# A transformer block's expert layer: every token through all eight experts, or each token's rows sent to its two

## The chip, the cores and the metric

The program runs on one core of a Trainium2 chip. The core has a matrix engine (TensorE, PE in the rows, its weight loads PEld), three engines for elementwise work (VectorE or DVE, ScalarE or ACT, GpSimd or POOL), and SyncE (SP), which issues transfers. The metric is the device time of one execution in microseconds, lower is better. The kernel before took 1424.11 us as the median of three runs (1423.81 to 1424.6).

## The reference

Two layers, each an attention and a feed-forward part with a residual. Only the last part, the mixture of experts of layer 1, is changed. It works on 32 x 128 = 4096 tokens of 128 numbers:

```python
gate_out = jnp.einsum('bsd,ed->bse', x, Wg)            # x: layer norm of the tokens
top_v, top_i = jax.lax.top_k(gate_out, K)              # K = 2 of E = 8 experts
probs = jax.nn.softmax(top_v, axis=-1)
for e in range(E):
    w_e = jnp.sum(probs * (top_i == e), axis=-1)       # 0 for 6 of the 8 experts
    h1 = jnp.einsum('bsd,hd->bsh', x, W1[e])           # H = 256
    h2 = jnp.einsum('bsd,hd->bsh', x, W2[e])
    g = h1 * jax.nn.sigmoid(h1) * h2
    out = out + jnp.einsum('bsh,dh->bsd', g, W3[e]) * w_e[..., None]
x = x + jnp.tanh(g_ffn[1]) * out
```

## The kernel before

The kernel is a row of stages: `setup`, `split_transposed` and `project0`, `attention0`, `feed_forward0`, a second `split_transposed`, `attention1`, a third `split_transposed`, `mixture`. Each stage is one block of instruction streams, one for each engine that has work in it. At its end all five engines meet at a barrier (line 89 of the helper `Memory`), SyncE too, also where it had nothing to do. Within a stage semaphores alone order the engines.

A matrix product is made in half precision three times over (high part by high, high by low, low by high), so each fp32 operand is split into a high and a low fp16 part.

The third `split_transposed` (1098.6 to about 1120 us) normalises the tokens on VectorE, turns 128 x 128 blocks on TensorE and leaves them in `xh` and `xl`, features on the partitions. `mixture` takes eight chunks of 512 tokens (CH = 4 sequences), and for each chunk all eight experts. For one chunk and expert, TensorE makes 12 products of 512 columns (`rise`, lines 1628 to 1630), ScalarE the tanh and the high part, VectorE two products (lines 1753 and 1761), GpSimd the low part (line 1583), and TensorE 24 products of 128 columns (`fall`, line 1642). VectorE weighs the result by the gate, which is zero for six experts of eight (line 1771), and GpSimd adds it to `X` (line 1578). The gate of the next chunk is worked out on VectorE between two experts. SyncE only stores the finished chunks (line 1605). Everything stays in the on-chip memory, and the loops over the chunks are hardware loops.

SyncE's queue is empty from the end of `setup` to `attention1`, whose transposes (lines 1219 and 1222) move fp16 tiles within the on-chip memory. GpSimd issues no transfer in this kernel.

## Time and profile before

| | |
|---|---|
| median of three runs | 1424.11 us |
| the profiled execution: its own time | 1424.81 us |
| its span in the trace | 1423.0 us |
| TensorE busy, mean granted clock | 1213.8 us (85%), 0.883 |
| VectorE, ScalarE, GpSimd busy | 1075.0, 928.7, 855.5 us |
| data moved by transfers | 30.97 MB |

The span is the time from the first to the last instruction in the trace, 1.8 us less than the execution's own time. A busy engine is not always at its peak: matmuls overlap, so an engine that is 85% busy can have room. Times in the rows are microseconds from the span's start.

### The profile page before, as it was taken

What the parts mean: (1) busy time and instruction counts of PE and PEld (TensorE: products, weight loads), DVE (VectorE), ACT (ScalarE), POOL (GpSimd) and SP (SyncE); (2) the same over time, 40 slices, a digit from 0 to 9 for tenths busy, and PEclk for the clock granted to TensorE, in tenths of its full rate; (3) what the DMA queues carried; (4) which work ended last, traced back from release to release, by engine and by line L of the source; (5) the groups of instructions that cost most, each with busy time, mean ns of one, the idle gap of its engine ahead of it and who ended that gap; (6) DMA issues with size and microseconds to landing.
All of it is one profiled execution on the core that took longest, in us unless ns stands there. A gap on an engine that the chain in (4) does not pass through costs nothing. (4 is left out here: it accounts for less than half of the span.)

```text
span 1423.0 us, 39532 instructions
## 1 busy us (share of the span) xinstructions
PE 1213.8 (85%) x14773; PEld 910.6 (64%) x14773; DVE 1075.0 (76%) x2878; ACT 928.7 (65%) x1858; POOL 855.5 (60%) x823
## 2 busy tenths in 40 slices
PE   1578999958994599999999999999994688888887
PEld 1445777745663388878787878787874355555555
DVE  5888666666988766676868676867774799999996
ACT  0678888845663488878787878787872445554554
POOL 0251888852115366666666666666663477777778
PEclk9678555558996699999999999999997699999998
DMA  9100000000000011112211121112111000000000
GB/s 234 46 1 1 2 3 2 3 1 1 1 1 1 1 24 32 32 32 31 28 29 32 32 32 32 28 30 29 32 32 23 1 1 9 8 7 7 7 8 16
DMA packets 93785, 30.97 MB, mean 22 GB/s; under 512 B 78227, under 2 KB 91963, under 8 KB 93627
## 3 DMA queue, kind: packets, MB, share of 16 engines
q1 hardware_dynamic: 82587, 25.40, 8.8%
q10 hardware_dynamic: 11040, 3.42, 1.1%
q8 instruction: 106, 1.74, 0.5%
q14 instruction: 52, 0.43, 0.1%
HBM read 9.92 MB, written 2.10 MB: 8 GB/s over the span
## 5 line engine op out<-in xcount | busy, mean ns | idle before, releaser
L1167 POOL TENSOR_TENSOR attention_pl_l<-attention_probs_l,attention_ph_l 128x512 f16<-128x512 f32 x128 | 148.1, 1157 | 181.0 <-ACT attention_ph_l L1337 181.0
L1401 DVE TENSOR_REDUCE attention_negmax<-bank 128x2 f16<-128x410 f32 x256 | 137.7, 579 | 136.5 <-PE bank L1246 136.3
L1583 POOL TENSOR_TENSOR mixture_hidden_l<-mixture_hidden,mixture_hidden_h 128x512 f16<-128x512 f32 x128 | 148.2, 1158 | 74.9 <-ACT mixture_hidden_h L1670 74.9
L610 POOL TENSOR_TENSOR attention_probs_l<-attention_probs,attention_probs_h 77x512 f16<-77x512 f32 x128 | 145.1, 1152 | 65.6 <-ACT attention_probs_h L689 61.5
L1167 POOL TENSOR_TENSOR attention_pl_c<-attention_probs_c,attention_ph_c 77x512 f16<-77x512 f32 x128 | 147.5, 1152 | 0.0
L1679 ACT ACTIVATE mixture_tanh<-bank 128x512 f32<-128x512 f32 x128 | 76.4, 597 | 105.6 <-PE bank L1630 105.6
L1628 PE MATMUL bank<-mixture_xs,moeh 128*128 128x512 f16 x256 | 98.2, 384 | 31.6 <-DVE mixture_hidden L1761 31.6
L1261 PEld LDWEIGHTS bank<-identh,attention_negmax 128*128 128x128 f16 (+1 forms) x1024 | 83.3, 107 | 55.7
L1229 PE MATMUL bank<-layer_kv,ah 128*128 128x128 f16 x1024 | 108.7, 220 | 11.1 <-PEq L89 11.0
L1337 ACT ACTIVATE attention_probs_l<-bank 128x512 f32<-128x512 f32 x128 | 76.4, 597 | 56.9 <-PE bank L1261 56.9
L1257 PE MATMUL bank<-attention_th,layer_kv 128*128 128x512 f16 (+1 forms) x256 | 97.0, 379 | 14.6 <-issue 14.5
L1229 PE MATMUL bank<-v1h,layer_kv 128*128 128x256 f16 (+1 forms) x512 | 106.3, 275 | 1.1 <-DVE attention_vl_c L1408 1.1
L1395 DVE SCALAR_TENSOR_TENSOR attention_tl<-bank,attention_th 128x512 f16<-128x512 f32 x128 | 87.8, 686 | 17.6 <-ACT attention_th L1328 17.6
L1753 DVE SCALAR_TENSOR_TENSOR mixture_half<-mixture_tanh,bank 128x512 f32<-128x512 f32 x128 | 87.3, 682 | 15.4 <-ACT mixture_tanh L1679 15.3
L1261 PE MATMUL bank<-identh,attention_negmax 128*128 128x128 f16 (+1 forms) x1024 | 98.9, 219 | 0.0
L1630 PE MATMUL bank<-mixture_xs,moeh 128*128 128x512 f16 x256 | 97.8, 382 | 0.0
L1629 PE MATMUL bank<-mixture_xs,moel 128*128 128x512 f16 x256 | 97.8, 382 | 0.0
L1275 PE MATMUL bank<-attention_vh_l,attention_ph_l 128*128 128x65 f16 x512 | 95.7, 195 | 2.0 <-POOL attention_pl_c L1167 2.0
L688 ACT ACTIVATE attention_probs<-bank 77x512 f32<-77x512 f32 x128 | 75.7, 591 | 33.0 <-PE bank L634 30.5
L1259 PE MATMUL bank<-attention_tl,layer_kv 128*128 128x512 f16 (+1 forms) x256 | 97.0, 379 | 0.0
L1258 PE MATMUL bank<-attention_th,layer_kv 128*128 128x512 f16 (+1 forms) x256 | 97.0, 379 | 0.0
L1275 PE MATMUL bank<-attention_vh_c,attention_ph_c 77*128 77x65 f16 x512 | 95.9, 195 | 0.0
(327 smaller groups left out, 4813.2 us busy)
## 6 DMA issues: line engine op xcount, KB each, us to landing
X<-in_x SPq DMA_DIRECT2D x4, 512.0 KB, 9.2
out<-X SPq DMA_DIRECT2D x8, 256.0 KB, 2.3
ctx<-in_ctx SPq DMA_DIRECT2D x1, 1232.0 KB
setup_nat_w<-in_w SPq DMA_DIRECT2D x1, 1024.0 KB, 14.3
attention_turned_h<-attention_heads_h SPq DMA_TRANSPOSE x64, 2.4
attention_turned_l<-attention_heads_l SPq DMA_TRANSPOSE x64, 2.4
setup_nat_f<-in_fw ACTq DMA_DIRECT2D x2, 256.0 KB, 7.0
setup_nat_q<-in_q ACTq DMA_DIRECT2D x1, 512.0 KB, 8.0
```

Source lines behind the costliest of these rows:

```text
L610: pool.tensor_tensor(probs_l[:, n % SLOTS], probs[:, n % 2], probs_h[:, n % SLOTS], ALU.subtract).then_inc(p_split, 1)
L1167: last = pool.tensor_tensor(low[:, g % 2], whole[:, g % 2], high[:, g % 2], ALU.subtract)
L1229: last = pe.matmul(dst, x, y, start=i == 0, stop=i == 2)
L1257: pe.matmul(dst, kh, th[:, g], start=True, stop=False)
L1258: pe.matmul(dst, kl, th[:, g], start=False, stop=False)
L1261: last = pe.matmul(dst[:, h], negmax[:, g, h:h + 1].broadcast_to([S, width]), w.identh[:], start=False, stop=h == HG - 1)
L1275: last = pe.matmul(mix[:, h], x, y, start=i == 0, stop=i == len(products) - 1)
L1401: last = dve.tensor_reduce(negmax[:, g, 2 * i:2 * i + 2], score[i], AX.X, ALU.max, negate=True)
L1583: pool.tensor_tensor(hidden_l[:, e % 4, j], hidden[:, e % 2, j], hidden_h[:, e % 4, j], ALU.subtract).then_inc(hid_lo, 1)
L1628: pe.matmul(dst, wh, xs[:, u, 0], start=True, stop=False)
L1629: pe.matmul(dst, wl, xs[:, u, 0], start=False, stop=False)
L1630: last = pe.matmul(dst, wh, xs[:, u, 1], start=False, stop=True)
```

## The change

The mixture no longer runs all experts on all tokens. A stage `route` normalises the tokens, works out the gates, and counts for each token its place in the list of its first and of its second expert (two more matrix products with a triangle and with ones). It then writes two copies of each token, high and low part and a number of its own, to `tokens`, a buffer in the chip's main memory with a region of 4096 rows for each expert; a row has 272 fp16 numbers, 544 bytes. Each write is an indirect transfer of GpSimd with 128 rows, one place for each partition; there are 2 x 4 of them for a chunk and 64 in all. A table tells for each of 71 tiles of 128 rows which expert it belongs to and where it begins.

The stage `experts` goes through the 71 tiles. SyncE reads the tile's first row from the table into a register, brings the tile in by a transfer that transposes it, and the rows' numbers by a second one. TensorE reads the expert from the table, once for `rise` and once for `fall`, and takes the weights at an address from the register. The work for a tile is 12 products of 128 columns and 6 more, a quarter of what it was for a chunk and expert. GpSimd sends the 128 rows of the result by an indirect transfer to `outputs`, each to the place of its token and choice. Then both results of each token are read back, weighed on VectorE and ScalarE, and added to `X` by VectorE and GpSimd.

Before all this, `tokens` is cleared: SyncE writes 33664 blank rows of 544 bytes (18.3 MB) in the stage `project0`. All three lists below are instructions in program order. The names in brackets are semaphores; a name such as `setup_hi_done` is that of an earlier user of the same semaphore.

GpSimd in one step of the expert loop before: low parts and sums.

```order
L1583 TENSOR_TENSOR mixture_hidden_l<-mixture_hidden,mixture_hidden_h 128x512 [waits mixture_hid_hi]
L1574 REGISTER_ALU
L1578 TENSOR_TENSOR X<-X,mixture_part 128x512 [waits mixture_combined,mixture_added]
L1582 REGISTER_ALU
L1583 TENSOR_TENSOR mixture_hidden_l<-mixture_hidden,mixture_hidden_h 128x512 [waits mixture_hid_hi]
```

GpSimd now, for one chunk of `route` (fill the payload, send) and one tile of `experts`:

```order
L1658 IOTA route_pay 128x8 [waits setup_made]
L1660 TENSOR_TENSOR route_pay<-route_normed,route_pay 128x8x128
L1672 DMA tokens<-route_pay,route_slot 33664x272 [waits setup_tanh_done,setup_summed,setup_chain]
L1672 DMA tokens<-route_pay,route_slot 33664x272 x7
...
L1943 TENSOR_TENSOR experts_hidden_l<-experts_hidden,experts_hidden_h 128x256 [waits setup_pchain]
L1948 DMA outputs<-experts_y_rows,experts_ids 8192x128 [waits id_in0,experts_y_copied]
```

The sums have gone from GpSimd's loop, and 64 and 71 indirect transfers have come.

SyncE in the same stage, before:

```order
L1602 UNCONDITIONAL_BRANCH
L1602 ISA
L1605 ISA [waits mixture_added]
L1605 DMA out<-X 128x4x128
L1602 REGISTER_ALU
L1602 COMPARE_AND_BRANCH
```

SyncE now, one tile of 71 (`setup_hi_done` stands for the end of `rise` four tiles earlier, `y_out0` for the landing of a result eight tiles earlier):

```order
L1818 TENSOR_LOAD table
L1818 ISA x2
L1821 ISA [waits setup_hi_done]
L1821 DMA_TRANSPOSE experts_xt<-tokens 128x2x128
L1824 ISA [waits y_out0]
L1824 DMA experts_ids<-tokens 128x2
```

The transpose of the next tile is queued behind this wait for `y_out0`.

TensorE before, the end of a `rise` and the start of a `fall`, with no register load:

```order
L1628 MATMUL bank<-mixture_xs,moeh 128x512
...
L1642 MATMUL bank<-w3h,mixture_hidden_h 128x128 [waits mixture_combined,mixture_hid_lo]
L1642 MATMUL bank<-w3l,mixture_hidden_h 128x128
```

TensorE now, from the end of a `fall` into the next `rise`:

```order
L1862 MATMUL bank<-w3l,experts_hidden_h 128x128
L1862 MATMUL bank<-w3h,experts_hidden_l 128x128
L1867 TENSOR_LOAD table
L1867 ISA x2
L1852 ISA [waits setup_mask_done,x_in2]
L1852 MATMUL bank<-experts_xt,moeh 128x128
L1852 REGISTER_ALU
L1852 MATMUL bank<-experts_xt,moel 128x128
L1852 MATMUL bank<-experts_xt,moeh 128x128
```

A register load stands ahead of each `rise` and of each `fall`, 142 in all.

The diff, cut to its core:

```diff
+ROW = 2 * 128 + 16
+TILES = (2 * B * S + E * (S - 1)) // S
+ROWS = E * B * S + (TILES - 2 * B) * S
+NOWHERE = 1 << 20
...
+        @block.sync
+        def _(sp):
+            sp.dma_start(w.tokens.rearrange("(t p) r -> p t r", p=128),
+                         w.blank[:].unsqueeze(1).broadcast_to([128, ROWS // 128, ROW])).then_inc(w.cleared, 16)
...
-            def add(k, e):
-                n = k * E + e
-                rows = w.X[:, bass.ds(k * CH, CH), :]
-                pool.wait_ge(combined, n + 1)
-                if late(n):
-                    pool.wait_ge(added, n)
-                pool.sem_inc(pool_waited, 1)
-                pool.tensor_tensor(rows, rows, part[:, e % 2], ALU.add).then_inc(added, 1)
...
+            def pay_high(k):
+                act.wait_ge(normed_in, k + 1)
+                if k >= 2:
+                    act.wait_ge(sent[k % 2], 16 * 2 * CH * (k // 2))
+                act.activation(pay[:, k % 2, :, :, 0:D], normed[:, k % 2].unsqueeze(1).broadcast_to([S, 2, CH, D]),
+                               ACT.Copy).then_inc(pay_hi, 1)
...
+            def fill(k):
+                u = k % 2
+                pool.wait_ge(pay_hi, k + 1)
+                pool.iota(pay[:, u].bitcast(INT32)[:, :, :, D:D + 1].rearrange("p i c o -> p i (c o)"),
+                          pattern=[[1, 2], [2 * S, CH]], base=2 * S * CH * k, channel_multiplier=2).then_inc(numbered, 1)
+                pool.tensor_tensor(pay[:, u, :, :, D:2 * D], normed[:, u].unsqueeze(1).broadcast_to([S, 2, CH, D]),
+                                   pay[:, u, :, :, 0:D], ALU.subtract).then_inc(pay_lo, 1)
+            def send(k):
+                u = k % 2
+                if k == 0:
+                    pool.wait_ge(w.cleared, 16)
+                pool.wait_ge(slots_in, k + 1)
+                pool.wait_ge(numbered, k + 1)
+                pool.wait_ge(pay_lo, k + 1)
+                for i in range(2):
+                    for c in range(CH):
+                        pool.indirect_dma_start(w.tokens, bass.IndirectOffsetOnAxis(ap=slot[:, u, i, c:c + 1], axis=0),
+                                                pay[:, u, i, c], None).then_inc(sent[u], 16)
+            pool.memset(pay[:, :, :, :, 2 * D + 2:ROW].rearrange("p u i c r -> p (u i c) r"), 0.0).then_inc(padded, 1)
+            fill(0)
+            pool.wait_ge(padded, 1)
+            for k in range(NCH):
+                if k + 1 < NCH:
+                    fill(k + 1)
+                send(k)
+            for u in range(2):
+                pool.wait_ge(sent[u], 16 * 2 * CH * (NCH // 2))
...
+            def normalise(k):
+                if k >= 2:
+                    dve.wait_ge(turned, k - 1)
+                    dve.wait_ge(pay_lo, k - 1)
+                for c in range(CH):
+                    b = CH * k + c
+                    last = dve.tensor_scalar(normed[:, k % 2, c], w.X[:, b], w.mv[:, b, 0:1], w.rstd[:, b:b + 1],
+                                             ALU.subtract, ALU.mult)
+                last.then_inc(normed_in, 1)
...
+            def places(k):
+                u = k % 2
+                dve.wait_ge(ranked, k + 1)
+                last = dve.tensor_tensor(spot[:], rank, w.region[:].unsqueeze(1).broadcast_to([S, CH, E]), ALU.add)
+                last.then_inc(rank_read, 1)
+                dve.wait_ge(rank_read, k + 1)
+                for i in range(2):
+                    last = dve.tensor_tensor(is_it[:, i], is_it[:, i], spot[:], ALU.mult)
+                link(last)
+                link(dve.tensor_reduce(place[:], is_it[:], AX.X, ALU.add))
+                if k >= 2:
+                    dve.wait_ge(sent[u], 16 * 2 * CH * (k // 2))
+                dve.tensor_copy(slot[:, u], place[:]).then_inc(slots_in, 1)
...
+            for n in range(TILES):
+                row = sp.value_load(w.table[0:1, 0, n:n + 1], min_val=0, max_val=ROWS - S)
+                if n >= RX:
+                    sp.wait_ge(h_done, n - RX + 1)
+                sp.dma_start_transpose(xt[:, n % RX], w.tokens[bass.ds(row, S), 0:2 * D]).then_inc(x_in[n % RX], 16)
+                if n >= RI:
+                    sp.wait_ge(y_out[(n - RI) % RY], 16 * ((n - RI) // RY + 1))
+                sp.dma_start(ids[:, n % RI], w.tokens[bass.ds(row, S), 2 * D:2 * D + 2]).then_inc(id_in[n % RI], 16)
+            for i in range(RY):
+                sp.wait_ge(y_out[i], 16 * used(RY, i, TILES))
+            back = w.outputs.rearrange("(b s i) d -> s b i d", s=S, i=2)
+            for k in range(NCH):
+                rows = slice(CH * k, CH * k + CH)
+                if k >= 2:
+                    sp.wait_ge(summed, k - 1)
+                    sp.wait_ge(scaled, k - 1)
+                sp.dma_start(both[:, k % 2], back[:, rows]).then_inc(both_in[k % 2], 16)
+                if k:
+                    sp.wait_ge(finished, k)
+                    done = slice(CH * (k - 1), CH * k)
+                    sp.dma_start(a["out"].rearrange("b s d -> s b d")[:, done], w.X[:, done]).then_inc(stored, 16)
+            sp.wait_ge(finished, NCH)
+            sp.dma_start(a["out"].rearrange("b s d -> s b d")[:, B - CH:B], w.X[:, B - CH:B]).then_inc(stored, 16)
+            sp.wait_ge(stored, 16 * NCH)
...
+            def rise(n, first):
+                pe.wait_ge(x_in[n % RX], 16 * (n // RX + 1))
+                if n >= 2:
+                    pe.wait_ge(hid_in, n - 1)
+                for dst, i in ((h1[n % 2], 0), (h2[n % 2], 1)):
+                    for j in range(MH):
+                        wh, wl = (x[:, i, bass.ds(first + j, 1), :].rearrange("p o h -> p (o h)") for x in (w.moeh, w.moel))
+                        for k, (wt, x) in enumerate(((wh, 0), (wl, 0), (wh, 1))):
+                            last = pe.matmul(dst[:, j], wt, xt[:, n % RX, x], start=k == 0, stop=k == 2)
+                last.then_inc(h_done, 1)
+            def fall(n, first):
+                pe.wait_ge(hid_lo, n + 1)
+                if n >= 2:
+                    pe.wait_ge(y_copied, n - 1)
+                for j in range(MH):
+                    wh, wl = (x[:, bass.ds(first + j, 1), :].rearrange("p o d -> p (o d)") for x in (w.w3h, w.w3l))
+                    for k, (x, wt) in enumerate(((hidden_h, wh), (hidden_h, wl), (hidden_l, wh))):
+                        last = pe.matmul(y[n % 2], x[:, n % 4, j], wt, start=j == 0 and k == 0, stop=j == MH - 1 and k == 2)
+                last.then_inc(y_done, 1)
+            for n in range(TILES + LAG):
+                if n < TILES:
+                    rise(n, pe.value_load(w.table[0:1, 1, n:n + 1], min_val=0, max_val=MH * (E - 1)))
+                if n >= LAG:
+                    fall(n - LAG, pe.value_load(w.table[0:1, 1, n - LAG:n - LAG + 1], min_val=0, max_val=MH * (E - 1)))
...
+            def squash(n):
+                act.wait_ge(h_done, n + 1)
+                if n >= 2:
+                    act.wait_ge(halved, n - 1)
+                act.activation(tanh[:, n % 2], h1[n % 2], ACT.Tanh, scale=0.5 / WS).then_inc(tanhed, 1)
+            def hidden_high(n):
+                act.wait_ge(hid_in, n + 1)
+                if n >= 4:
+                    act.wait_ge(y_done, n - 3)
+                act.activation(hidden_h[:, n % 4], hidden[:, n % 2], ACT.Copy).then_inc(hid_hi, 1)
+            def copy_out(n):
+                act.wait_ge(y_done, n + 1)
+                if n >= RY:
+                    act.wait_ge(y_out[n % RY], 16 * (n // RY))
+                act.activation(y_rows[:, n % RY], y[n % 2], ACT.Copy).then_inc(y_copied, 1)
...
+            for n in range(TILES + LAG + 1):
+                if n < TILES:
+                    squash(n)
+                if 1 <= n < TILES + 1:
+                    hidden_high(n - 1)
+                if n >= LAG + 1:
+                    copy_out(n - LAG - 1)
+            for k in range(NCH):
+                scale_second(k)
...
+            def add_first(k):
+                dve.wait_ge(both_in[k % 2], 16 * (k // 2 + 1))
+                for c in range(CH):
+                    b = CH * k + c
+                    last = dve.scalar_tensor_tensor(w.X[:, b], both[:, k % 2, c, 0], w.share[:, b, 0:1], w.X[:, b],
+                                                    ALU.mult, ALU.add)
+                last.then_inc(summed, 1)
...
+            def hidden_low(n):
+                pool.wait_ge(hid_hi, n + 1)
+                pool.tensor_tensor(hidden_l[:, n % 4], hidden[:, n % 2], hidden_h[:, n % 4], ALU.subtract).then_inc(hid_lo, 1)
+            def send(n):
+                pool.wait_ge(y_copied, n + 1)
+                pool.wait_ge(id_in[n % RI], 16 * (n // RI + 1))
+                pool.indirect_dma_start(w.outputs, bass.IndirectOffsetOnAxis(ap=ids[:, n % RI].bitcast(UINT32), axis=0),
+                                        y_rows[:, n % RY], None, bounds_check=2 * B * S - 1,
+                                        oob_is_err=False).then_inc(y_out[n % RY], 16)
...
+            for n in range(TILES + LAG + 1):
+                if n < TILES:
+                    hidden_low(n)
+                if n >= LAG + 1:
+                    send(n - LAG - 1)
+            for k in range(NCH):
+                add_second(k)
...
+        nc.clear_and_free_semaphores(w.spent)
+        nc.all_engine_barrier()
+        route(nc, w, bank)
+        experts(nc, a, w, bank)
...
```

## Rows read from the trace of the kernel before

**Rows 1.** the page: busy time, and the granted clock in 40 slices

```profile
PE 1213.8 (85%) x14773; PEld 910.6 (64%) x14773; DVE 1075.0 (76%) x2878; ACT 928.7 (65%) x1858; POOL 855.5 (60%) x823
...
PEclk9678555558996699999999999999997699999998
```

**Rows 2.** windows (busy and count of five engines, clock, DMA share, GB/s): split, experts

```profile
1098.60:1120.20 21.60, 8.92 (x32) 5.73 (x32) 15.84 (x45) 8.66 (x16) 9.31 (x8) 0.50 0.00 0
1120.20:1421.00 300.80, 262.66 (x2368) 160.31 (x2368) 263.54 (x536) 150.51 (x264) 224.87 (x192) 0.98 0.02 7
```

**Rows 3.** groups by line and shape, 1120 to 1423 us: busy us, mean ns

```profile
L1583 POOL TENSOR_TENSOR mixture_hidden_l<-mixture_hidden,mixture_hidden_h 128x512 f16<-128x512 f32 x128 | 148.2, 1158 | 74.9 <-ACT mixture_hidden_h L1670 74.9
L1628 PE MATMUL bank<-mixture_xs,moeh 128*128 128x512 f16 x256 | 98.2, 384 | 31.6 <-DVE mixture_hidden L1761 31.6
...
L1642 PE MATMUL bank<-w3h,mixture_hidden_h 128*128 128x128 f16 x512 | 89.8, 220 | 1.9 <-POOL mixture_hidden_l L1583 1.9
...
L1725 DVE TENSOR_TENSOR mixture_diff<-mixture_top 128x4 f32<-128x4 f32 x8 | 7.7, 958 | 0.3
```

**Rows 4.** timeline, VectorE: first routing chain of the stage

```profile
1121.26 0.23 DVE L1708 TENSOR_SCALAR mixture_gate<-bank 128x64 f32<-128x64 f32 x1 [0.48 <-PE bank L1615]
...
1123.26 0.17 DVE L1725 TENSOR_TENSOR mixture_diff<-mixture_top 128x4 f32<-128x4 f32 x1
...
1125.54 0.19 DVE L1746 TENSOR_TENSOR mixture_weight<-mixture_is 128x32 f32<-128x32 f32 x1
```

**Rows 5.** line L184: SyncE's four loads of x, 512 KB each, min/median/max ns

```profile
L184 SPq DMA_DIRECT2D X<-in_x x4: 458/1407/2561, 0.7 to 4.5; - x4
```

**Rows 6.** waits, SyncE: us in total, times, longest

```profile
SPq L191 <- DMA ctx<-in_ctx: 21.6, 1, 21.6
```

**Rows 7.** windows: the loads, then the stage `project0`

```profile
0.00:40.00 40.00, 4.21 (x20) 3.83 (x20) 21.67 (x114) 4.16 (x11) 4.37 (x15) 0.95 0.99 242
86.00:132.90 46.90, 43.15 (x288) 24.39 (x288) 40.03 (x96) 40.62 (x96) 9.53 (x8) 0.95 0.00 1
```

**Rows 8.** timeline, TensorE: the first matmul behind `project0`

```profile
133.85 0.31 PE L619 MATMUL bank<-layer_kst,layer_qst 32*128 32x77 f16 x8 [2.30 <-PEq L89]
```

**Rows 9.** line L1219: SyncE's transposes

```profile
L1219 SPq DMA_TRANSPOSE attention_turned_h<-attention_heads_h x64: 1189/1192/2461, 508.7 to 1083.7; - x64
...
DMA to landing us min/median/max: 2.3/2.4/4.8
```

**Rows 10.** line L1605: SyncE's stores of X, 256 KB each

```profile
L1605 SPq DMA_DIRECT2D out<-X x8: 378/379/445, 1177.2 to 1420.3; - x8
...
DMA to landing us min/median/max: 2.3/2.3/3.5
```

**Rows 11.** timeline, ScalarE's queue: a load of 128 rows

```profile
0.74 0.43 ACTq L196 DMA_DIRECT2D setup_gates<-in_gx  x1
```

**Rows 12.** groups by shape, ScalarE: 256, 128 and 1024 columns

```profile
L1349 ACT ACTIVATE attention_vh_l<-bank 128x256 f16<-128x256 f32 x128 | 49.4, 386 | 44.5 <-PE bank L1229 40.4
...
L1364 ACT ACTIVATE attention_out<-bank 128x128 f32<-128x128 f32 x32 | 8.9, 277 | 27.2 <-PE bank L1293 27.2
...
L229 ACT ACTIVATE v1h<-setup_nat_v 128x1024 f16<-128x1024 f32 x1 | 1.1, 1057 | 4.3 <-DMA setup_nat_o<-in_o 4.3
```

**Rows 13.** groups by shape, VectorE: 256 columns, and normalising 128

```profile
L1418 DVE TENSOR_TENSOR attention_heads_out<-bank,attention_recip 128x256 f32<-128x256 f32 x128 | 54.3, 425 | 4.4
...
L416 DVE TENSOR_SCALAR split_normed_x<-X,mv,rstd 128x128 f32 x96 | 40.3, 488 | 4.5 <-PEq L441 1.8 <-PE bank L438 1.2 <-issue 1.0
```

**Rows 14.** groups by shape, GpSimd: 308 columns

```profile
L467 POOL TENSOR_TENSOR rows_cl<-split_whole_ctx,rows_ch 128x308 f16<-128x308 f32 x8 | 6.0, 769 | 0.6 <-ACT rows_ch L453 0.6
```

**Rows 15.** timeline, TensorE: spacing of 128-column matmuls at the lower clock

```profile
1082.77 0.31 PE L1293 MATMUL bank<-o1h,attention_turned_l 128*128 128x128 f16 x1
1082.88 0.31 PE L1293 MATMUL bank<-o1h,attention_turned_h 128*128 128x128 f16 x1
```

418 lines of the change are left out of this document (215 added, 203 removed).

## The prediction, made before the changed kernel ran

> **What bounds the kernel now.** I read the page first. TensorE is busy for 85% of the span and the granted clock is at its upper level, 2.4 GHz, from the 33rd slice on [rows 1]. That is a mean over stages, and the change touches the last two, so I read those by windows. The third `split_transposed` lasts 21.6 us at the lower clock, 1.2 GHz. The expert stage runs 300.8 us at 0.98 of the full clock, with TensorE busy for 262.7, VectorE for 263.5 and GpSimd for 224.9 us, and 7 GB/s moved [rows 2]. Then I read the expert stage by groups. The 512-column matmuls take 0.38 us each, overlapping, the wait before the first of a group is for VectorE's last product and adds 31.6 us, and GpSimd's low part takes 1.16 us, 128 times [rows 3]. The stage is thus a tight pipeline of TensorE and VectorE, about 4.7 us for each of 64 pairs of chunk and expert, and transfers play no part in it. Everything from 1098.6 us to the span's end at 1423.0 us, 324 us in all, is replaced.
>
> **What goes.** The arithmetic falls to 71 tiles of 128 rows from 256 (32 sequences by 8 experts), a factor of 3.6. VectorE's two products are then 71 x 2 x 0.425 us [rows 13] = 60 us, ScalarE's three operations 71 x (0.386 + 0.386 + 0.277) [rows 12] = 74 us. TensorE's 18 products of 128 columns for a tile start 0.107 us apart at the lower clock [rows 15], 1.9 us for a tile, and half that at the upper one. None of these would fill 324 us. What comes instead is latency and the issuing of small transfers, and the sum is made of these.
>
> **Two prices that no row shows.** An indirect transfer of 128 rows issued by GpSimd: the lower bound is ScalarE's issue of a plain 128-row load, 0.43 us [rows 11]; the upper is the longest issue of a transpose on SyncE, 2.46 us [rows 9]. The nearest row is the usual transpose issue of 1.19 us, also one instruction that makes addresses for 128 partitions, and here a place must be read for each. I take 1.3 us. A register load from on-chip memory: it is at most a transfer's landing, 2.3 us [rows 10], and at least 0.16 us, about a smallest VectorE instruction [rows 4]. I take 0.7 us, near the geometric mean, and know it badly.
>
> **The clearing write.** 18.3 MB are added in `project0`. Nothing waits for the data until `route`, a thousand microseconds later. But SyncE must have issued them before it can reach the barrier at the stage's end. The loads at the start show how issuing behaves: a load of 512 KB took 0.46 us to issue when the queues were empty and up to 2.56 us once they were full [rows 5], which is 205 GB/s, the pace of the data. When SyncE had issued its last load, 21.6 us of transfers were still ahead [rows 6], part of them ScalarE's. At 242 GB/s, the rate of the full queues, the write takes 76 us, of which 10 to 20 may still be queued when SyncE is free. `project0` lasts 47 us [rows 7] and the next matmul starts 1 us behind it [rows 8]. So the barrier is late by 76 - 10 - 47 = 19 us; I take 20. The lower end is 0, if the queue takes all descriptors at once. The upper end is 95 us, if 544-byte writes run at half the rate (152 - 10 - 47). The extra memsets of `setup` cost nothing, since GpSimd's stream waits there for the loads anyway.
>
> **Route.** The first chunk is a chain: inverse root on VectorE 2.6 us (twelve small operations at 0.2 to 0.23 us [rows 4]), eight normalisations of 0.3 to 0.49 us [rows 13], turning, high part 0.6, low part 0.7, gates, and the chain of small VectorE operations, 4.5 us from the first to the last in the old stage [rows 4], with about 1.5 us more for the places. With the payload's copy on ScalarE and subtraction on GpSimd between them I get 18 us to the first indirect write.
> From then on GpSimd has a loop of its own. `pay_high(k+1)` on ScalarE waits until the eight writes of chunk k-1 have landed (2.3 us, as a store of X [rows 10]), copies 1024 columns (1.06 us [rows 12]), and only then can GpSimd subtract 1024 columns (twice a 512-column one of 1.16 us [rows 3], 2.3 us) and issue the next eight. With the hops that is 5.8 + 8 x 1.3 = 16.2 us for a chunk. VectorE's work for a chunk, about 9 us, lies beside it. Route: 18 + 7 x 16.2 + 10.4 + 2.3 = 144 us. Two barriers and the clearing of semaphores: 3 us.
>
> **Experts.** For one tile each engine needs:
> GpSimd: a subtraction of 256 columns, between 308 columns at 0.77 us and nothing, so 0.64 [rows 14], one indirect write of 1.3 and hops of 0.2 = 2.1 us.
> SyncE: register load 0.7, transpose 1.19 for four blocks [rows 9], so perhaps 0.9 for two, the numbers 0.43 [rows 11], checks 0.1 = 2.1 us.
> TensorE: 1.9 us of products at the lower clock beside two register loads of 0.7 which partly overlap, 2 to 3.3 us.
> But a circle is longer. SyncE waits with the numbers of tile n until the result of tile n-8 has landed, and the transpose of n+1 is queued behind that wait. Result landed -> numbers 0.43 -> register load 0.7 -> transpose landed 2.4 [rows 9] -> `rise` 1.3 (12 x 0.107) -> tanh, two products, high and low part 2.3 with six hops of 0.1 -> GpSimd's previous write 1.3 -> the write of result n-3, 1.3 -> landed 2.3: 12.6 us for five tiles, 2.5 us each. I take 2.5: 71 x 2.5 = 178 us, and 12 us to fill and drain the chain. Total 190 us.
>
> **Reading back.** 4.2 MB come in and 2.1 MB go out after the last tile. At 242 GB/s [rows 7] that is 26 us, with a first and a last landing 30 us; VectorE's four products and GpSimd's addition of 1.3 us lie beside it. The sum for the end of the kernel is 144 + 3 + 190 + 30 = 367 us for 324.
>
> **Sum.** 1424.8 us of the profiled execution + 367 - 324 + 20 = 1488 us. The median was 0.7 us below the profiled execution, so 1487 us, 4% slower.
>
> A sentence beside it on the skill: DMA: Bandwidth & Descriptors in the Trainium skill, Anatomy of one DMA, says that a GpSimd-issued DMA has a fixed part of about 2.0 us, mostly the receipt of the last write, and its rules for kernel authors say that a transfer under 64 KB pays mostly overhead. The trace agrees for other engines' transfers, 2.3 to 2.4 us to land [rows 9, 10]; with 2.0 for my 2.3 the circle would be 2.4 us a tile and the sum 5 us less. It speaks against this change, whose 270-odd transfers are 64 KB or 68 KB or less.
>
> **Rival B: the indirect writes are cheap (faster).** If a write takes 0.7 us and a register load 0.2, the chunk of `route` is 5.8 + 5.6 = 11.4 us and the stage 106 instead of 144. The circle falls to 10.2 us, 2.0 us a tile, 36 us less. With a stall of 10 instead of 20 us for the clearing: 1487 - 38 - 36 - 10 = 1403 us. For it: ScalarE's plain issue is 0.43 us. Against: places are data here. The point from which it decides is a write below about 0.9 us with a tile below 2.1 us.
>
> **Rival C: register loads bound TensorE.** A load of 1.2 us, the price of SyncE's address work [rows 9], that TensorE cannot overlap, gives 2 x 1.2 and a part of 1.9 us of products, 3.5 us a tile: 71 us more, 1558 us. For it: two loads stand in TensorE's stream for each tile, and its waits behind each. Against: queued matmuls may run under them.
> The Trainium skill, Runtime: NRT & Kernel Launch, The ~15µs preamble/postamble breakdown, gives about 1.3 us for `TENSOR_LOAD`, there from main memory; no row here shows one.
>
> **Rival D: the write is held up by VectorE.** Small VectorE operations took 0.96 us in the expert stage [rows 3] and 0.17 us when GpSimd was idle [rows 4], so the two hold each other up. If a write is held by as much, it takes 2.1 to 2.2 us: `route` 58 us more, a tile 3.0 us (0.64 + 2.2 + 0.2), 36 us more, 1581 us.
> The Trainium skill, SBUF — State Buffer, SBUF: two separate sides, states this mechanism: while VectorE runs in a two-port mode GpSimd cannot write its descriptors. That VectorE and GpSimd wait for each other is in the trace; for descriptors no run shows it yet.
>
> **Rival E: the clearing stalls for long.** At half the rate the barrier is 95 us late, 1562 us. The blank rows are written in order from one source, which speaks for the full rate.
>
> **How the numbers follow.** Forecast 0.42 (its own range 1445 to 1530), B 0.23, C 0.13, D 0.14, E 0.08. The range is 1395 to 1590: it holds B's time and D's, and leaves out a better B and C with D together. A change below 0.2% (3 us) cannot be told from none. B crosses 1424 only if nearly all of it holds, but part of the forecast's low tail lies there too: faster 0.23, same 0.02, slower 0.75.
>
> **What would show it.** In the profile after: the first matmul of `attention0` 10 to 30 us later than 133.9 us, with all engines idle before it; eight indirect writes of a chunk 10 us apart from first to last and `route` 130 to 160 us; GpSimd waiting at each chunk for ScalarE's copy; a tile every 2.5 us, with the transposes queued behind the wait for a landed result; TensorE below half busy and mostly at 1.2 GHz. A write of 0.7 us or less, or a tile under 2 us, would make the forecast wrong, and so would a barrier behind `project0` that is on time.

## The result, and the profile after

| kernel | median, us | lowest to highest, us | profiled execution, us | span, us |
|---|---|---|---|---|
| before | 1424.36 | 1423.81 to 1424.9 | 1424.8 | 1423.0 |
| changed | 1512.27 | 1511.81 to 1512.76 | 1512.76 | 1511.0 |

The change made the kernel slower by 6.2%: the ratio is 1.0618, 95% interval 1.0603 to 1.0632. The prediction was 1487 us in a range of 1395 to 1590 us, so the direction and the range hold, and the likeliest value is 25 us short.

The page of the changed kernel, busy time and granted clock, answers to [rows 1]:

```profile
PE 1118.1 (74%) x13787; PEld 872.4 (58%) x13787; DVE 927.7 (61%) x2780; ACT 855.6 (57%) x1847; POOL 832.3 (55%) x864
...
PEclk9678555569985999999999999999955555555555
```

TensorE is busy 96 us less, and the clock never comes back to its upper level after the 29th slice: the whole new part runs at 1.2 GHz, where the old expert stage had run at 0.98 of 2.4 GHz [rows 2]. By windows (busy time and count of PE, PEld, DVE, ACT, POOL, then clock, DMA share, GB/s):

```profile
1098.00:1120.00 22.00, 5.40 (x49) 4.28 (x49) 16.42 (x78) 3.78 (x6) 8.52 (x8) 0.50 0.03 10
1120.00:1240.00 120.00, 6.81 (x87) 5.91 (x87) 47.83 (x228) 9.54 (x18) 72.42 (x72) 0.50 0.10 36
1264.00:1472.00 208.00, 154.13 (x1188) 110.76 (x1188) 54.91 (x131) 57.16 (x200) 113.67 (x138) 0.50 0.20 42
1472.00:1509.00 37.00, 0.00 (x0) 0.00 (x0) 10.19 (x32) 10.22 (x32) 10.60 (x9) 0.50 0.55 170
```

First `route` up to its first write, then its writes, then the steady part of `experts`, then reading back. The boundaries are the first register load of `experts` (1242.6 us) and the first load of reading back (1473.8 us), so that from 1098.6 us on the new part takes 144 + 231 + 37 = 412 us against 324 us before, and that is the whole difference of the spans (88.0 us).

**The clearing write.** SyncE's one instruction (min/median/max ns), its landing (KB, median us), and TensorE's first matmul behind `project0`, which answers to [rows 8]:

```profile
L514 SPq DMA_DIRECT2D tokens<-blank x1: 409/409/409, 86.0 to 86.0; - x1
```

```profile
tokens<-blank SPq DMA_DIRECT2D x1, 17884.0 KB, 70.7
```

```profile
134.52 0.32 PE L644 MATMUL bank<-layer_kst,layer_qst 32*128 32x77 f16 x8 [2.31 <-PEq L93]
```

It was issued in 0.41 us, the data (18.3 MB; the view's KB are of 1024 bytes) took 70.7 us, and `attention0` began 0.7 us later than before. No stall.

**Route.** The timeline of one chunk's end (start, duration, engine; in brackets what the engine waited for):

```profile
1157.38 0.97 POOL L1672 DMA_INDIRECT tokens<-route_pay,route_slot  x1 [0.30 <-issue]
1159.76 1.06 ACT L1636 ACTIVATE route_pay<-route_normed 128x1024 f16<-128x1024 f32 x1 [15.07 <-DMA tokens<-route_pay,route_slot]
1160.72 0.19 ACT L1641 ACTIVATE route_expd<-route_diff 128x4 f32<-128x4 f32 x1
...
1160.94 0.17 DVE L1730 TENSOR_SCALAR route_p<-route_expd 128x4 f32<-128x4 f32 x1 [8.99 <-ACT route_expd L1641]
1160.99 2.11 POOL L1660 TENSOR_TENSOR route_pay<-route_normed,route_pay 128x1024 f16<-128x1024 f32 x1
...
1161.36 1.77 DVE L1732 TENSOR_SCALAR share<-route_p,moe_out 128x4 f32<-128x4 f32 x1
1163.17 0.23 DVE L1733 TENSOR_SCALAR share<-share,moe_out 128x4 f32<-128x4 f32 x1
```

```profile
1165.15 0.99 POOL L1672 DMA_INDIRECT tokens<-route_pay,route_slot  x1 [2.04 <-DVE route_slot L1747]
```

The last of eight writes ends at 1158.35, has landed at 1159.7, and only then does ScalarE copy the payload; GpSimd subtracts; VectorE's places come 2.04 us behind it, because the exponential stood behind the payload's copy on ScalarE and because a VectorE operation of 4 columns took 1.77 us while GpSimd was subtracting; it ended 0.03 us after the subtraction did. Eight writes, then 6.8 us of preparation, 16.7 us for a chunk in the middle. A write, in `route` and in `experts`:

```profile
L1672 POOL DMA_INDIRECT tokens<-route_pay,route_slot x64: 954/969/1417, 1114.8 to 1234.6; - x64
```

```profile
L1948 POOL DMA_INDIRECT outputs<-experts_y_rows,experts_ids x71: 969/989/1016, 1264.5 to 1471.5; - x71
```

With the 0.30 us between two of them a write in `route` is 1.27 us. The first starts at 1114.8 us, 17.4 us after the stage's first instruction at 1097.4.

**Experts.** TensorE's stream of two successive tiles:

```profile
1319.10 0.31 PE L1862 MATMUL bank<-w3h,experts_hidden_l 128*128 x1
1319.85 0.28 PE L1852 MATMUL bank<-experts_xt,moeh 128*128 128x128 f16 x1 [0.43 <-DVE experts_hidden L1922]
...
1320.99 0.31 PE L1852 MATMUL bank<-experts_xt,moeh 128*128 128x128 f16 x1
1321.61 0.29 PE L1862 MATMUL bank<-w3h,experts_hidden_h 128*128 x1 [0.30 <-issue]
...
1322.13 0.31 PE L1862 MATMUL bank<-w3h,experts_hidden_l 128*128 x1
1322.89 0.29 PE L1852 MATMUL bank<-experts_xt,moeh 128*128 128x128 f16 x1 [0.45 <-DVE experts_hidden L1922]
```

Twelve products of the rise start about 0.107 us apart, as in [rows 15] (1.14 us from first to last), then nothing starts for 0.62 us, then come six products of the fall (0.52 us), then nothing for 0.76 us: 3.04 us to the next rise. In both gaps stand the instructions of one register load (min/median/max ns; the other line, L1869, has nearly the same numbers):

```profile
L1867 PEldq TENSOR_LOAD <-table x71: 297/304/476, 1242.7 to 1460.6; - x71
L1867 PEldq FUSED_REGOPS  x71: 151/151/171, 1243.3 to 1461.0; - x71
L1867 PEldq SEQ_ASSERT  x71: 18/18/28, 1243.5 to 1461.2; - x71
```

0.30 us of load, 0.15 of register work and 0.02 of check are 0.47 us, and the array runs dry beneath them. The view of waits puts the second gap down to VectorE's product, which came last by the profile but is not what ends it; the experiments decide that. SyncE's own waits (us in total, times, longest) show the circle of the prediction, short here:

```profile
SPq L1824 <- DMA outputs<-experts_y_rows,experts_ids: 31.0, 48, 1.2
```

From the 11th to the 61st result write (1295.23 and 1449.23 us) a tile takes 3.08 us. This number, called the tile below, is taken in the same way from every trace.

**Reading back.** The chain that ended last (start, duration, what it was):

```profile
1474.24 4.92 DMA experts_both<-outputs
1479.18 2.23 DVE X L1929 x4
1481.47 1.27 POOL X L1956
1483.24 4.74 DMA experts_both<-outputs
```

A load, its use and the next load alternate: with two buffers, the load of chunk k+2 waits until chunk k has been added.

### The profile page after: what moved, and what is told of

The parts are those of the page before. It is cut to its first block and busy times, and to the rows that moved or that the text cites. A ratio compares the mean times of both kernels' runs of the same rounds, so it can differ in the third digit from the quotient of the medians.

```text
span 1511.0 us, 38558 instructions
## 1 busy us (share of the span) xinstructions
PE 1118.1 (74%) x13787; PEld 872.4 (58%) x13787; DVE 927.7 (61%) x2780; ACT 855.6 (57%) x1847; POOL 832.3 (55%) x864
## 5 line engine op out<-in xcount | busy, mean ns | idle before, releaser
L1852 PE MATMUL bank<-experts_xt,moeh 128*128 128x128 f16 x568 | 104.5, 310 | 60.8 <-DMA experts_xt<-tokens 31.4
L1916 DVE SCALAR_TENSOR_TENSOR experts_half<-experts_tanh,bank 128x256 f32<-128x256 f32 x71 | 29.9, 421 | 176.5 <-ACT experts_tanh L1877 176.5
L1877 ACT ACTIVATE experts_tanh<-bank 128x256 f32<-128x256 f32 x71 | 27.3, 384 | 187.8 <-PE bank L1852 183.3
L1852 PEld LDWEIGHTS bank<-experts_xt,moeh 128*128 x568 | 69.0, 130 | 80.4 <-issue 79.3
L1282 PE MATMUL bank<-attention_th,layer_kv 128*128 128x512 f16 (+1 forms) x256 | 97.0, 379 | 12.9 <-issue 12.6
L1943 POOL TENSOR_TENSOR experts_hidden_l<-experts_hidden,experts_hidden_h 128x256 f16<-128x256 f32 x71 | 46.9, 661 | 107.7 <-ACT experts_hidden_h L1883 107.7
L1300 PE MATMUL bank<-attention_vl_l,attention_ph_l 128*128 128x65 f16 x512 | 95.6, 192 | 0.0
L1300 PE MATMUL bank<-attention_vh_c,attention_pl_c 77*128 77x65 f16 x512 | 95.5, 192 | 0.0
## 6 DMA issues: line engine op xcount, KB each, us to landing
tokens<-blank SPq DMA_DIRECT2D x1, 17884.0 KB, 70.7
```

Source lines behind the costliest of these rows:

```text
L1282: pe.matmul(dst, kh, th[:, g], start=True, stop=False)
L1300: last = pe.matmul(mix[:, h], x, y, start=i == 0, stop=i == len(products) - 1)
L1852: last = pe.matmul(dst[:, j], wt, xt[:, n % RX, x], start=k == 0, stop=k == 2)
```

## The experiments

All times are medians; the ratio is to the kernel before, with its 95% interval. "Tile" and "chunk" are as above; the clock is the mean granted clock from 1270 to 1380 us. The kernel before, run again beside them, took 1424.4 to 1425.5 us, so a difference of about 1 us in the third column means nothing.

| kernel | us | against changed | ratio to before | tile, us | clock |
|---|---|---|---|---|---|
| changed | 1512.27 | | 1.0618 (1.0603 to 1.0632) | 3.08 | 0.50 |
| e_pe_const | 1487.39 | -24.9 | 1.0437 (1.0419 to 1.0454) | 2.72 | 0.74 |
| e_one_load | 1490.79 | -21.5 | 1.0462 (1.0444 to 1.0479) | 2.67 | 0.75 |
| e_three_loads | 1558.04 | +45.8 | 1.0932 (1.0914 to 1.0951) | 3.74 | 0.50 |
| e_unchecked | 1490.78 | -21.5 | 1.0451 (1.0433 to 1.0468) | 2.74 | 0.72 |
| e_rings | 1513.72 | +1.5 | 1.0623 (1.0605 to 1.0641) | 3.08 | 0.50 |
| e_batch_both | 1482.64 | -29.6 | 1.0400 (1.0383 to 1.0417) | 2.64 | 0.77 |
| e_batch_rings | 1468.60 | -43.7 | 1.0307 (1.0292 to 1.0321) | 2.45 | 0.80 |
| e_act_order | 1502.60 | -9.7 | 1.0546 (1.0528 to 1.0563) | 3.08 | 0.50 |
| e_pay4_act | 1486.73 | -25.5 | 1.0434 (1.0417 to 1.0452) | 3.08 | 0.50 |
| e_clear_double | 1513.14 | +0.9 | 1.0620 (1.0602 to 1.0638) | 3.08 | 0.50 |
| e_all | 1432.89 | -79.4 | 1.0047 (1.0035 to 1.0059) | 2.47 | 0.83 |
| e_best | 1401.68 | -110.6 | 0.9834 (0.9820 to 0.9847) | 2.17 | 0.84 |

### What bounds the experts: register loads or the circle

Theory L: the two register loads in TensorE's stream stop it. Rival: the prediction's circle over SyncE and the landed results.

**e_pe_const**

```diff
-                    rise(n, pe.value_load(w.table[0:1, 1, n:n + 1], min_val=0, max_val=MH * (E - 1)))
+                    rise(n, MH * (n * E // TILES))
...
-                    fall(n - LAG, pe.value_load(w.table[0:1, 1, n - LAG:n - LAG + 1], ...))
+                    fall(n - LAG, MH * ((n - LAG) * E // TILES))
```

This kernel leaves the choice of the weights out, so its result is not the layer's; only its time is of use.

> TensorE takes the expert of a tile as a constant (expert 9n/71 style, tiles spread evenly) and reads no register in the expert stage; the routing of weights is left out, all sizes, waits and transfers stay. Theory L (the two register loads of a tile stop TensorE, about 0.56 us of idle array each, beside 18 x 0.107 us of products = 3.05 us a tile): a tile falls to the next limit, GpSimd's 0.66 + 0.99 + hops or SyncE's issues, 2.1 to 2.3 us, so 1440 to 1460 us. The prediction's circle over SyncE and landed results: a tile stays near 3.07 us, 1509 to 1515 us.

**e_one_load**

```diff
+                    at[n] = pe.value_load(w.table[0:1, 1, n:n + 1], min_val=0, max_val=MH * (E - 1))
+                    rise(n, at[n])
...
+                    fall(n - LAG, at.pop(n - LAG))
```

> One register load a tile on TensorE instead of two: the number loaded for the rise is kept in its register and used again for the fall three tiles later. Theory L: 0.56 us less a tile, 71 x 0.56 = 40 us, 1472 us (1465 to 1480). The circle: TensorE's loads lie in slack, 1509 to 1515 us.

**e_three_loads**

```diff
                 if n < TILES:
+                    pe.value_load(w.table[0:1, 1, n:n + 1], min_val=0, max_val=MH * (E - 1))
```

> A third register load a tile on TensorE, its value unused. Theory L: 71 x about 0.47 to 0.56 us more, 1545 to 1555 us. The circle: no change, 1509 to 1515 us.

**e_rings**

```diff
-("id_in", 8), ("y_out", 4)
+("id_in", 12), ("y_out", 6)
```

> The ring of slot numbers holds 12 tiles instead of 8 and that of result rows 6 instead of 4, so that SyncE waits with the numbers of tile n for result n-12 and ScalarE for result n-6. Theory L: SyncE's and ScalarE's waits for landed results shrink and nothing else changes, 1509 to 1515 us. The circle: seven or more tiles instead of five over the same way, 71 x 0.5 to 0.9 us less, 1450 to 1477 us.

The four agree on the changed kernel. Wider rings alone change neither the tile (3.08 us) nor the time by more than 1.5 us, so the circle does not bound it. A load more costs 0.66 us a tile, at the same clock (0.50 in both): the 0.47 us of its instructions and some more. That is above the 0.47 to 0.56 us expected. A load less is worth 0.41 us, and both loads less only 0.36 us. Theory L named the limit; its size for taking loads away was missed by half (1440 to 1460 expected, 1487 measured), because another limit waits at 2.65 to 2.7 us. The trace of e_pe_const shows which: SyncE's own stream.

```profile
1318.97 1.20 SPq L1821 DMA_TRANSPOSE experts_xt<-tokens  x1
1320.35 0.43 SPq L1824 DMA_DIRECT2D experts_ids<-tokens  x1
1321.51 1.18 SPq L1821 DMA_TRANSPOSE experts_xt<-tokens  x1
1322.87 0.43 SPq L1824 DMA_DIRECT2D experts_ids<-tokens  x1
```

```profile
PE bank L1852 <- DMA experts_xt<-tokens: 42.3, 32, 3.4
```

A transpose of 1.19 us, 0.19 us, the slot numbers in 0.43 us, and 0.72 us for the register load, its check and the address are 2.53 us a tile. From 1270 to 1390 us the median distance of two transposes is 2.55 us, in e_one_load too, and SyncE waits for a landed result before only 6 of about 44 slot numbers (3 us in all). TensorE meanwhile waits 42.3 us of 110 for transposed rows (second fence). The circle is thus not the limit here either. This is read from the trace: no run took out SyncE's part alone with the wider rings.

The clock moves as well: with both loads gone TensorE is granted 0.74 of full speed instead of 0.50. The window of e_one_load, with one load gone:

```profile
1270.00:1380.00 110.00, 78.38 (x749) 64.47 (x750) 34.49 (x82) 35.01 (x123) 67.92 (x83) 0.75 0.24 50
```

So what one load costs can't be read from the kernels without it; only e_three_loads gives a price.

**e_unchecked**

```diff
-                    rise(n, pe.value_load(w.table[0:1, 1, n:n + 1], min_val=0, max_val=MH * (E - 1)))
+                    rise(n, number(n))        # the same load, skip_runtime_bounds_check_because=...
```

> The changed kernel with TensorE's two register loads a tile as before, but without the check of each number against its bounds (0.15 us of register work and 0.02 us for the check in the trace, twice a tile). If load and check both lie in TensorE's stream uncovered, a tile falls from 3.08 by 0.34 to 2.74 us, 71 x 0.34 = 24 us less, 1486 to 1491 us, just at the 2.65 to 2.7 us of the circle behind it. Rival: only the load stops TensorE and the checks run under queued products, 1509 to 1515 us.

The tile is 2.74 us as expected: the checks lie in the open too. The clock rose as well (0.50 to 0.72), so not all of the 0.34 us must be the checks' own. And SyncE's stream is close behind here too, its median step 2.56 us, so this run gives no exact price of a check.

### The limit behind it

**e_batch_both**: one load instruction for the numbers of four tiles.

```diff
+                if n % 4 == 0:
+                    many = min(4, TILES - n)
+                    _, got = nc.values_load_multi_w_load_instructions(
+                        w.table[0:1, 0, n:n + many], engines=(sp.engine,), min_val=0, max_val=ROWS - S)
+                    at.update(zip(range(n, n + many), got))
+                row = at.pop(n)
...
```

> TensorE and SyncE each load the numbers of four tiles with one instruction every fourth tile; TensorE uses each number for the rise and again for the fall. Everything else as in the changed kernel. With one load a tile the stage stopped at 2.7 us a tile, and its trace shows SyncE issuing without a wait: 1.18 us transpose, 0.19, 0.43 us for the slot numbers, 0.72 us of register load, checks and address, 2.5 us a tile. Theory S (SyncE is the next limit behind TensorE's loads): SyncE falls to about 2.1 to 2.2 us and a tile with it to 2.2 to 2.4 us, so 1455 to 1470 us. Rival (the transposes themselves, landing late beside the other transfers, hold TensorE): as with one load, 1485 to 1491 us. Rival 2 (a load costs by the numbers read, so one of four costs as four): 1500 us or more.

SyncE's batch, min/median/max ns:

```profile
L1821 SPq TENSOR_LOAD <-table x18: 221/305/731, 1243.5 to 1422.7; - x18
...
L1821 SPq FUSED_REGOPS  x71: 4/152/366, 1244.1 to 1424.0; - x71
```

A load of four numbers takes 0.305 us, one of a single number 0.274 to 0.304: rival 2 falls, the price is that of the instruction, but the checks are still made for each number. Theory S was right about the limit and wrong about what its removal brings: SyncE's stream is shorter now (three steps of 1.94 us, then one of 3.3 us or more with the batch's load), but the tile only fell from 2.67 to 2.64 us, and the time, 1482.6 us, is 2.4 us below the first rival's range. The next limit lay right behind. SyncE's stream, and one write of GpSimd's:

```profile
1321.46 1.17 SPq L1827 DMA_TRANSPOSE experts_xt<-tokens  x1
1322.81 0.44 SPq L1830 DMA_DIRECT2D experts_ids<-tokens  x1
1323.37 1.18 SPq L1827 DMA_TRANSPOSE experts_xt<-tokens  x1
1325.93 0.33 SPq L1830 DMA_DIRECT2D experts_ids<-tokens  x1
1328.32 1.36 SPq L1827 DMA_TRANSPOSE experts_xt<-tokens  x1
```

```profile
1323.35 0.99 POOL L1960 DMA_INDIRECT outputs<-experts_y_rows,experts_ids  x1 [0.16 <-issue]
```

Transposes can follow each other in 1.9 us, and here do. Then SyncE stands still from 1324.55 until it issues the slot numbers at 1325.93. GpSimd's write that began at 1323.35 has landed 2.3 us later, at 1325.7. That is the prediction's circle: the numbers of tile n behind the landed result of tile n-8, the next transpose queued behind them. From 1270 to 1390 us SyncE waits so before 10 of 45 slot numbers, 12.9 us in all or 0.29 us a tile. (Of the 2.06 us after it the batch's load, four checks and address work are 1.5 us, the least that this step takes at any batch; what the rest is, the trace does not say.)

**e_batch_rings**: e_batch_both and e_rings together.

```diff
-("id_in", 8), ("y_out", 4)
+("id_in", 12), ("y_out", 6)
```

> The loads of four numbers at a time on both engines, and the rings of e_rings (slot numbers 12 tiles, result rows 6 tiles). With the loads cut alone, three kernels stopped at 2.65 to 2.7 us a tile whatever was cut (constants, one load, batches), and the trace of the last shows SyncE issuing three or four transposes at once and then idle, 4 tiles in 10.9 us. Theory K (the prediction's circle is the second limit: numbers of tile n behind the landed result of tile n-8, the next transpose behind them, which TensorE's loads had covered): the wider rings free it, and a tile falls to GpSimd's 0.66 + 0.16 + 0.99 + 0.05 or TensorE's 1.93 + 0.25, 2.1 to 2.3 us, 1445 to 1460 us. Rival T (transposes and their landing set 2.65 us by themselves): no change from 1482.6, 1478 to 1486 us.

The same edit that was worth nothing in the changed kernel is worth 14.0 us here, and SyncE's view of waits has no wait left in this stretch. Theory K holds in direction for this kernel, though the three kernels of its text were not held by the circle alone: SyncE's stream held the first two. The tile stops at 2.45 us instead of 2.1 to 2.3. SyncE's stream, now without a wait, has a mean step of 2.41 us, of which the check of each number is 0.17 us.

### Route

**e_act_order**

```diff
             for k in range(NCH):
-                if k + 1 < NCH:
-                    pay_high(k + 1)
                 gate_exp(k)
                 if k + 2 < NCH:
                     rows_high(k + 2)
+                if k + 1 < NCH:
+                    pay_high(k + 1)
```

> In route, ScalarE takes the exponential of a chunk and the high part two chunks on before the payload's copy, which waits for landed writes; ring of payloads unchanged at 2. Theory R (the trace of the changed kernel: writes end, 1.4 us until landed, 1.06 us copy, 0.14 + 2.11 us on GpSimd, then 2.0 us of waiting for VectorE's places, which were queued behind the exponential and then behind GpSimd's subtraction): the 2.0 us a chunk go, 7 x 2.0 = 14 us less, 1495 to 1501 us. Rival (the places are late for another reason, or the landing alone sets the loop): 1509 to 1515 us.

9.7 us less, where 14 were expected. Six chunks paid the wait for places, not seven (VectorE's places were waited for 11.7 us, 6 times, in the changed kernel). From the first of the 64 writes to the last it is 108.3 us instead of 119.8, 11.5 us less. The profiled run began the stage 1.6 us later (1098.95 us), before anything that this edit touches.

**e_pay4_act**

```diff
-                if k >= 2:
-                    act.wait_ge(sent[k % 2], 16 * 2 * CH * (k // 2))
-                act.activation(pay[:, k % 2, :, :, 0:D], ...
+                if k >= 4:
+                    act.wait_ge(sent[k % 4], 16 * 2 * CH * (k // 4))
+                act.activation(pay[:, k % 4, :, :, 0:D], ...
```

> ScalarE's order as in e_act_order, and rings of 4 instead of 2 for the payloads and places, so that no copy waits for the writes of the chunk two before it. Theory R: landing and copy leave the loop as well; a chunk of GpSimd is 0.14 + 2.11 + 8 x 1.27 + 0.2 = 12.6 us against 16.8, 7 x 4.2 = 29 us less, 1480 to 1487 us. Rival W (the writes are a queue that drains no faster than one in 1.6 us or more, so GpSimd is then held at its issues): the eight writes last longer than 10.2 us, 1495 to 1512 us.

25.5 us less. GpSimd's timeline at a chunk's end now has no wait for ScalarE or VectorE:

```profile
1148.89 0.97 POOL L1673 DMA_INDIRECT tokens<-route_pay,route_slot  x1 [0.30 <-issue]
1149.88 0.16 POOL L1659 IOTA route_pay<- 128x8 int32 x1
1149.99 2.12 POOL L1661 TENSOR_TENSOR route_pay<-route_normed,route_pay 128x1024 f16<-128x1024 f32 x1
1152.28 0.99 POOL L1673 DMA_INDIRECT tokens<-route_pay,route_slot  x1 [0.17 <-issue]
```

The next chunk's first write starts at 1164.63, 12.35 us later: 2.3 us of filling and eight writes. Theory R holds for the loop; rival W falls, the writes stay 1.27 us apart when nothing else is in the way. Seven times 4.2 us were expected; only six chunks have the long step, since nothing is filled before the last chunk's writes.

### The clearing write

**e_clear_double**

```diff
-        w.tokens = nc.dram_tensor("tokens", (ROWS, ROW), FP16).ap()
+        w.tokens = nc.dram_tensor("tokens", (2 * ROWS, ROW), FP16).ap()
...
-                         w.blank[:].unsqueeze(1).broadcast_to([128, ROWS // 128, ROW]))
+                         w.blank[:].unsqueeze(1).broadcast_to([128, 2 * ROWS // 128, ROW]))
```

> The region table in DRAM is twice as large and the clearing write with it, 36.6 MB; nothing reads the second half. Theory P (the prediction's: issuing goes at the pace of the data once the queues are full): the barrier behind project0 is 70 us or more late, 1580 us or more. Theory Q (the trace of the changed kernel: the issue took 0.41 us, the data 70.7 us): the data take 141 us beside attention0, which reads nothing from DRAM, 1509 to 1516 us.

```profile
tokens<-blank SPq DMA_DIRECT2D x1, 35768.0 KB, 142.4
```

Twice the data (36.6 MB) take twice the time to land, and the kernel 0.9 us more, which is within the spread; the issue took 0.76 us. Theory Q.

### All together

**e_all**: e_pay4_act, e_batch_rings, and four buffers for reading back.

```diff
-                if k >= 2:
-                    sp.wait_ge(summed, k - 1)
-                    sp.wait_ge(scaled, k - 1)
-                sp.dma_start(both[:, k % 2], back[:, rows]).then_inc(both_in[k % 2], 16)
+                if k >= 4:
+                    sp.wait_ge(summed, k - 3)
+                    sp.wait_ge(scaled, k - 3)
+                sp.dma_start(both[:, k % 4], back[:, rows]).then_inc(both_in[k % 4], 16)
...
```

> All of it together: e_pay4_act's rings of 4 and ScalarE's order in route, e_batch_rings' loads and rings in experts, and a ring of 4 instead of 2 chunks for reading back, with the stores three chunks behind the loads. If the parts add: route 25 us less, experts as theory K says 60 us less, reading back 37 to about 30 us: 1512.5 - 25 - 60 - 7 = 1420 us, about the time of the kernel before (range 1410 to 1432). If rival T holds: 1512.5 - 25 - 30 - 7 = 1450 us.

1432.9 us, 0.5% above the kernel before. The parts add: 25.5 + 43.7 us, and from the last result write to the end 30.5 us instead of 39.5. Expected were 1420 us with a tile of 2.2 us; the tile is 2.47. Reading back now moves 234 GB/s instead of 170:

```profile
1405.00:1432.00 27.00, 0.00 (x0) 0.00 (x0) 14.63 (x32) 10.22 (x32) 10.22 (x8) 0.50 0.76 234
```

**e_best**: and three more steps.

```diff
-                pool.tensor_tensor(pay[:, v, :, :, D:2 * D], normed[:, u]..., pay[:, v, :, :, 0:D], ALU.subtract)
+                dve.tensor_tensor(pay[:, k % 4, :, :, D:2 * D], normed[:, k % 2]..., ...)    # behind places(k - 1)
...
-                pool.tensor_tensor(hidden_l[:, n % 4], hidden[:, n % 2], hidden_h[:, n % 4], ALU.subtract)
+                dve.tensor_tensor(hidden_l[:, n % 4], hidden[:, n % 2], hidden_h[:, n % 4], ALU.subtract)    # one tile later
...
+                        skip_runtime_bounds_check_because="the table is clamped where it is made")    # TensorE, SyncE
```

> e_all and three more steps. The payload's low part goes from GpSimd (0.16 + 2.12 us of a 12.4 us chunk) to VectorE, behind the places of the chunk; the low part of a tile goes from GpSimd (0.66 us) to VectorE; and the numbers loaded four at a time are no longer checked one by one (0.15 + 0.02 us for each on TensorE and on SyncE). Theory (GpSimd sets route, SyncE with 2.4 us and TensorE with 2.2 us a tile the experts): route 8 x 2.1 = 17 us less if VectorE's chunk stays under GpSimd's 10.4 us; a tile 2.4 to about 2.1 us, 71 x 0.3 = 21 us less: 1432.9 - 17 - 21 = 1395 us (1388 to 1408), 2% below the kernel before. Rival (VectorE's chunk, 9 us and the subtraction held up by GpSimd's writes, becomes the limit of route; transposes cannot be issued faster than one in 2.4 us): 1425 to 1435 us.

1401.7 us: 1.7% faster than the kernel before, against 1395 expected. By stages, against e_all: the 64 writes of `route` take 83.1 us from first to last start instead of 93.1, and a tile 2.17 us instead of 2.47. The 17 us expected in `route` were 10. GpSimd's writes now follow each other across a chunk's end, but 12 of the 64 are longer (1.03 to 1.74 us), ten of them beside VectorE's new subtraction or its normalising. The last two lines are the longest such case:

```profile
1134.72 0.96 POOL L1671 DMA_INDIRECT tokens<-route_pay,route_slot  x1 [0.31 <-issue]
1135.70 0.16 POOL L1659 IOTA route_pay<- 128x8 int32 x1
1136.02 0.98 POOL L1671 DMA_INDIRECT tokens<-route_pay,route_slot  x1 [0.16 <-issue]
...
1159.20 1.23 DVE L1700 TENSOR_TENSOR route_pay<-route_normed,route_pay 128x1024 f16<-128x1024 f32 x1 [0.36 <-ACT route_pay L1636]
1159.52 1.74 POOL L1671 DMA_INDIRECT tokens<-route_pay,route_slot  x1 [0.30 <-issue]
```

The three steps were not run one by one, so their shares within a stage are not separated.

## Why the prediction was right, and where its terms were not

| term | predicted, us | measured, us |
|---|---|---|
| stall behind the clearing write, `route` and barriers, from 1098.6 us | 20 + 147 | 144 |
| `experts` | 190 | 231 |
| reading back | 30 | 37 |
| sum, against 324 before | 387 | 412 |

**Direction: right, and mostly for the reason given.** The arithmetic fell as counted. What came in its place filled 412 us. In `route` and in reading back this was latency and the issuing of small transfers, as predicted; in `experts` it was register loads in TensorE's stream. Without these loads e_pe_const is still 4.4% slower than before, so the direction does not hang on them. None of the transfers is short of bandwidth: 10 to 42 GB/s until reading back.

**Clearing write: wrong.** The step was that issuing goes at the pace of the data once the queues are full, taken from the 512 KB loads with issues up to 2.56 us [rows 5]. This write of 18.3 MB took 0.41 us to issue, twice as much data 0.76 us. The lower bound (0) was the case. The landing, 76 us predicted, was 70.7. Why the loads were slow to issue and this write was not stays open.

**Route: the loop as described, its size in part by luck.** First write after 17.4 us (18), a write 1.27 us (1.3, chosen from [rows 9]), a chunk in the middle 16.7 us (16.2). Payload copy and landing were on the path, as e_pay4_act showed. The step missed is VectorE's: its work for a chunk was said to lie beside the writes, but its places came 2.04 us late. Two errors hid this. A write lands 2.3 us after its start, so 1.35 us after its end, while the sum added 2.3 us behind a whole write. And the sum counts the long step seven times; six chunks have it, and the last step is 10.9 us. From the stage's start to the last landing it was 139.5 us (144 predicted), and the change to `experts` took 5.7 us (3 predicted).

**Experts: the wrong limit.** The prediction said that the circle of 12.6 us for five tiles bounds the stage, 2.5 us a tile, and that TensorE's two register loads "partly overlap" its products. They do not. The gaps at the two loads, 0.62 and 0.76 us where products alone would follow in 0.107, turn 1.9 us of products into 3.04. This is rival C's mechanism with a cheaper load, 0.47 us of instructions and 0.66 us in effect instead of 1.2. The prediction had put TensorE at 2 to 3.3 us a tile and then compared the engines by their lower ends. Two terms with overlapping ranges should have been carried as a maximum, which costs more than either guess. SyncE's stream was too low as well, 2.1 us against 2.53: a transpose took 1.19 us here too, not 0.9, and 0.19 us behind it were left out. With TensorE's loads cut alone (e_pe_const, e_one_load), this stream was the limit, at 2.72 and 2.67 us a tile. The circle was real, but it held the tile only in e_batch_both, at 2.64 us, where the wider rings freed it. That three limits lie between 2.5 and 2.75 us is why the predicted 2.5 looks close. The circle's sum holds the landing added behind a whole write, about 1 us too much, and its size by itself was not measured. The Trainium skill, Runtime: NRT & Kernel Launch, The ~15µs preamble/postamble breakdown, gives about 1.3 us for a `TENSOR_LOAD` from main memory; from on-chip memory the trace has 0.27 to 0.30 us, and the measurement decides here.

**Reading back: the size was off.** 26 us of data at full rate were right for four buffers (30.5 us from the last write, of which 2.3 are its landing). With two buffers load and use alternate, and the rate was 170 GB/s.

**Rival B** needed writes below 0.9 us; they were 1.27. Its own sum was off: 12.6 us less twice 0.6 and 0.5 is a circle of 10.9 us and not 10.2, so 2.2 us a tile and about 1415 us instead of 1403. **Rival D** expected every write to be held up by VectorE. In the changed kernel a write takes 0.97 us in the median; six of 64 take 1.05 to 1.42 us, the longest beside VectorE operations on rows of 568 numbers, and in e_best one takes 1.74 us, which ends 0.83 us after the VectorE subtraction beside it. So the hold-up is there and rare. It was larger the other way, 1.77 us for a 4-column VectorE operation while GpSimd subtracted. The Trainium skill, SBUF — State Buffer, SBUF: two separate sides, ties the hold-up of writes to a two-port mode of VectorE. The longer writes agree with a hold-up, but no run here shows in which mode an operation ran. **Rival E** needed the stall, and there was none.

**Signs to look for.** The eight writes 10 us apart, `route` within 130 to 160 us, GpSimd waiting for ScalarE's copy at each chunk, and TensorE at 1.2 GHz throughout were seen. The late barrier and the tile of 2.5 us were not. TensorE below half busy was not seen in the steady part of `experts` either, where it was busy 154 of 208 us. The transposes did queue behind the wait for a landed result there (31.0 us in all), but e_rings shows that this did not bound the stage.

**The errors partly cancelled.** The stall and `route` were 23 us too long, 20 of them the stall that never came; `experts` was 41 and reading back 7 us too short: 25 us in sum. The total is nearer than its largest term, by luck.

## What to carry to other kernels

In this case a register load stood in full in TensorE's and in SyncE's instruction stream. Where numbers steer a short tile, load them several at a time, keep them in registers, and clamp the table so that no check is needed. When limits lie within their errors of each other, removing one is worth only the distance to the next, so look for all of them: TensorE's loads, SyncE's stream and the circle stood at 3.08, about 2.7 and 2.64 us here, and the wider rings were worth nothing alone and 14 us behind the loads. After each edit ask the trace which engine never waits. For a stage made of small transfers count the issues first, then every buffer whose reuse waits for a landing.
